# Slot steps of a four-layer graph kernel: index rows by DMA from DRAM, all diagonals on ScalarE, the variance ahead of the second normalisation, two buffers of powers

## What is computed

```python
m_j = h @ W1[:D];  m_i = h @ W1[D:]
pre = m_j[:, None, :, :] + m_i[:, :, None, :] + b1          # for every pair i, j
msg = gelu(layernorm(pre, g1, be1))
agg = einsum('bijo,bij->bio', msg, adjacency)
out = layernorm(concat([h, agg]) @ W2 + b2, g2, be2)
```

## Time and profile before

| | us |
|---|---|
| median of 3 runs (4080.77 to 4090.16) | 4087.21 |
| the profiled execution, device time | 4083.3 |
| its span, first to last instruction | 4081.4 |

### The profile page before, as it was taken

One profiled execution on the slowest core, in us unless ns is written; L12 is line 12 of the kernel. 1 busy time (PEld: TensorE's weight loads), 2 busy tenths in 40 slices (PEclk: granted clock), 3 DMA queues, 4 the chain that ended last, 5 costly groups with the idle time before them and its releaser, 6 DMA issues.

```text
span 4081.4 us, 93269 instructions
## 1 busy us (share of the span) xinstructions
PE 3302.0 (81%) x25274; PEld 2780.7 (68%) x25556; DVE 3378.2 (83%) x12271; ACT 2785.5 (68%) x6381; POOL 2108.6 (52%) x1923
## 2 busy tenths in 40 slices
PE   3484688887888888888798888888887887988898
PEld 2273567677676777767677776767776676776777
DVE  4788888898888888888888888888898888887830
ACT  2484676858667586776858676685868768595753
POOL 1182663718547292753729274471827547192730
PEclk7596899989899999999999999999999999999999
DMA  2000001000010100001010000101000010000000
GB/s 81 26 1 26 1 1 42 1 22 21 1 43 1 43 0 22 22 1 43 1 35 9 22 22 1 43 1 43 0 22 22 1 43 1 27 0 1 16 1 21
DMA packets 95513, 73.89 MB, mean 18 GB/s; under 512 B 7504, under 2 KB 95184, under 8 KB 95184
## 3 DMA queue, kind: packets, MB, share of 16 engines
q1 hardware_dynamic: 95184, 70.09, 5.7%
HBM read 61.68 MB, written 8.39 MB: 17 GB/s over the span
## 4 chain that ended last, share of the span: by engine, by line
issue 26%; POOL 25%; DVE 21%; PE 16%; ACT 6%; DVEq 3%; POOLq 2%; ACTq 0%; DMA 0%; SPq 0%
POOL v_z L511 18%; POOL v_diag L517 3%; PE n_bank_d L1599 3%; PE n_bank_d L1600 3%; PE n_bank_c L1582 3%; DVE v_normed L971 2%; PE n_bank_d L1596 2%; POOL v_prstd L525 2%; DVE v_top_at L1043 2%; PE n_bank_b L1660 1%; DVE v_top L1040 1%; PE n_bank_d L1496 1%; ACT v_pair L842 1%; DVE v_adj_x L1048 1%; POOLq L532 1%
## 5 line engine op out<-in xcount | busy, mean ns | idle before, releaser
L511 POOL TENSOR_TENSOR v_z<-v_z,all_bc_L_gnn_be 128x512 f32<-128x512 f32 x620 | 786.2, 1269 | 22.0 <-DVE v_z L1093 22.0
L525 POOL TENSOR_TENSOR v_prstd<-v_pvar,all_neg_half 128x8 f32<-128x8 f32 x310 | 563.5, 1818 | 267.8 <-DVE v_pvar L1109 240.0
L1496 PE MATMUL n_bank_d<-v_diag,v_msg 128*128 128x128 f32 x4960 | 637.1, 284 | 32.2 <-ACT v_diag L740 32.2
L1496 PEld LDWEIGHTS n_bank_d<-v_diag,v_msg 128*128 128x128 f32 x4960 | 594.8, 197 | 35.2 <-ACT v_diag L740 35.2
L740 ACT ACTIVATE v_diag<-all_ident,v_value 128x128 f32<-128x128 f32 x1860 | 572.5, 386 | 0.0
L1485 PE MATMUL n_bank_b<-v_parts,v_onehot 128*128 128x128 f16 x5472 | 374.0, 224 | 152.6 <-ACT n_bank_b L682 152.6
L1485 PEld LDWEIGHTS n_bank_b<-v_parts,v_onehot 128*128 128x128 f16 x5472 | 332.7, 100 | 224.7 <-ACT n_bank_b L682 183.5
L1582 PE MATMUL n_bank_c<-all_l_wsd,v_fT 128*128 128x256 f32 x1792 | 449.1, 392 | 31.4 <-ACT v_adjT L667 28.9
L1485 PE MATMUL n_bank_c<-v_parts,v_onehot 128*128 128x128 f16 x4960 | 346.9, 226 | 141.7 <-ACT n_bank_c L682 141.6
L1485 PEld LDWEIGHTS n_bank_c<-v_parts,v_onehot 128*128 128x128 f16 x4960 | 308.6, 101 | 213.2 <-ACT n_bank_c L682 168.4
L677 ACT ACTIVATE v_fT<-n_bank_d,all_l_c 128x256 f32<-128x256 f32 x256 | 119.7, 474 | 447.1 <-PE n_bank_d L1600 446.9
(11 more groups left out here) (281 smaller groups left out, 7344.6 us busy)
## 6 DMA issues: line engine op xcount, KB each, us to landing
v_adj_l<-in_adj SPq DMA_DIRECT2D x128, 256.0 KB, 3.7
v_adj_x<-in_adj SPq DMA_DIRECT2D x64, 256.0 KB, 3.4
v_ring<-in_x SPq DMA_DIRECT2D x16, 512.0 KB, 5.9
out_x<-v_xout SPq DMA_DIRECT2D x64, 128.0 KB, 2.0
w_wu<-in_L_gnn_wu SPq DMA_DIRECT2D x4, 192.0 KB, 2.5
all_W<-in_L_gnn_W SPq DMA_DIRECT2D x2, 128.0 KB, 4.3
w_raw<-in_L_gnn_ws SPq DMA_DIRECT2D x1, 192.0 KB, 3.0
w_raw<-in_L_gnn_wd SPq DMA_DIRECT2D x1, 192.0 KB, 3.1
```

The costliest lines, as they stand in the source:

```text
L511: nc.gpsimd.tensor_tensor(z[par][:, units], z[par][:, units], wide(bc["L2_gnn_be1"])[:, units], ALU.add).then_inc(sem["z_ready"], 1)
L525: nc.gpsimd.tensor_tensor(prstd[:], pvar[:], minus_half, ALU.pow).then_inc(sem["prstd_ready"], 1)
L1496: ins = nc.tensor.matmul(ps_agg[:, u // NB, (u % NB) * P:(u % NB + 1) * P], msg[par][:, u], diag[par][:, u], start=False, stop=False, skip ...
```

## The change

- `spread_out` on PE and `keep_spread` on ACT are gone. After the index is turned, ACT keeps one chunk in SBUF, and SP stores it to a DRAM tensor `slot_rows` (row k is the index row of slot k, 2 KB). For each slot SP loads that row onto all 128 partitions (256 KB written) into one of two buffers of `spread`. The first two are loaded in the mix stage, behind the loads for slot taking and ahead of those for layer 0; the others in the slot stage, each when `pick` of the slot just before it is done.
- All eight diagonals are made by ACT.
- `prstd` has two buffers, and DVE forms `pvar` ahead of the second half's normalisation.
- ACT's order: seed half 0, Gelu half 1 of the slot before, seed half 1, Gelu half 0, eight diagonals.

```diff
+            def spread_out(slot, par):
+                sp.dma_start(spread[:, par], slot_rows[bass.ds(slot, 1)].broadcast_to((P, UNITS * P)))\
+                    .then_inc(spread_in[par], 16)
+
+            def first_spreads(a, again):
...
+                with sp.Fori(0, chunks) as c:
+                    sp.wait_ge(sem["index_kept"], first + c + 2)
...
+                    sp.dma_start(slot_rows[bass.ds(c * P, P)], indexT[:]).then_inc(index_stored, 16)
...
+                sp.wait_ge(index_stored, sp.snap(stored) * 16 + 16)
...
+                for par in range(2):
+                    spread_out(par, par)
+
+            def slots(a):
...
+                with sp.Fori(1, pairs + 1) as i:
+                    for par in range(2):
+                        sp.wait_ge(sem["onehot_ready"], before + (i * 2 + par))
...
+                        spread_out(i * 2 + par, par)
...
             with sp.Fori(1, GROUPS - 3) as g:
                 mix(g)
+                slots(g + 1)
...
-                def pool_step(par, step, slot, first=False):
+                def pool_step(par, step, first=False):
                     if not first:
                         shift(1 - par, step, 0)
                     pool.wait_ge(sem["pvar_ready"], step + 1)
-                    nc.gpsimd.tensor_tensor(prstd[:], pvar[:], minus_half, ALU.pow).then_inc(sem["prstd_ready"], 1)
+                    nc.gpsimd.tensor_tensor(prstd[:, par], pvar[:], minus_half, ALU.pow).then_inc(sem["prstd_ready"], 1)
                     if not first:
                         shift(1 - par, step, 1)
-                        diagonals(1 - par, step, slot - 1)
...
-                    for u in range(BY_ACT):
+                    for u in range(UNITS):
                         ins = nc.scalar.activation(diag[par][:, u], ident[:], ACT.Copy,
                                                    scale=value[:, u, bass.ds(slot, 1)])
...
+                def act_step(par, step, slot, second=False):
+                    act.wait_ge(sem["z_made"], step * 2 + 1)
+                    seed(1 - par, 0)
+                    if not second:
                         gelu(par, act.snap(step - 1), 1)
+                    act.wait_ge(sem["z_made"], step * 2 + 2)
+                    seed(1 - par, 1)
+                    gelu(1 - par, step, 0)
+                    diagonals(1 - par, step, slot - 1)
...
             def pick(ahead, par):
-                dve.wait_ge(sem["spread_kept"], ahead + 1)
+                dve.wait_ge(spread_in[par], (ahead + (2 - par)) * 8)
...
-                        if not first:
+                        if half_ == 0 and not first:
                             dve.wait_ge(sem["prstd_ready"], step + 1)
-                            dve.wait_ge(sem["msg_ready"], step * 2 + (half_ + 1))
-                            normalise(1 - par, half_)
+                            dve.wait_ge(sem["msg_ready"], step * 2 + 1)
+                            normalise(1 - par, 0)
                     dve.wait_ge(sem["stats_done"], step * 2 + 2)
                     v.tensor_scalar(pvar[:].rearrange("p (q u) -> p q u", u=2), pstats[:, par, :, :, 2], 1.0 / D, UP * UP * LN_EPS,
                                     ALU.mult, ALU.add).then_inc(sem["pvar_ready"], 1)
+                    if not first:
+                        dve.wait_ge(sem["msg_ready"], step * 2 + 2)
+                        normalise(1 - par, 1)
                     pick(dve.snap(step + g * 2 + 2), par)
```

More of the change, by code:

```diff
@@ L214 @@
 HALF = UNITS // 2
-BY_ACT = 6
 LOWEST = -3.4028235e38
@@ L270, in network @@
         node_of = plan.sb("node_of", [P, NB])
-        spread = plan.sb("spread", [P, UNITS * P], BF16)
+        spread = plan.sb("spread", [P, 2, UNITS * P], BF16)
         junk = plan.sb("junk", [P, 2, N], BF16)
@@ L367, in network @@
         x_in = s.sem("x_in")
+        index_stored = s.sem("index_stored")
+        spread_in = [s.sem(f"spread_in{i}") for i in range(2)]
         adj_in = [s.sem(f"adj_in{b}") for b in range(GB)]
@@ L426, in mix @@
                     load_extract(g + 2)
+                if l1:
+                    first_spreads(g + 1, again)
                 if l0:
@@ L456, in _ @@
             load_x(1)
-            mix(-1, l3=False)
+            mix(-1, l3=False, again=False)
+            slots(0)
             mix(0, l3=False)
+            slots(1)
             with sp.Fori(1, GROUPS - 3) as g:
                 mix(g)
+                slots(g + 1)
             mix(GROUPS - 3, l0=False)
+            slots(GROUPS - 2)
             mix(GROUPS - 2, extract=False, l0=False)
-            mix(GROUPS - 1, extract=False, l0=False)
-            mix(GROUPS, extract=False, l0=False, refill=False)
+            slots(GROUPS - 1)
+            mix(GROUPS - 1, extract=False, l0=False, l1=False)
+            mix(GROUPS, extract=False, l0=False, refill=False, l1=False)
             for b in range(GB):
@@ L697, in keep_index @@
                     act.wait_ge(sem["index_turned"], first + c + 1)
-                    nc.scalar.activation(indexT[:, bass.ds(c, 1)].rearrange("p a n -> p (a n)"), ps_index,
-                                         ACT.Copy).then_inc(sem["index_kept"], 1)
+                    act.wait_ge(index_stored, (first + c) * 16 + 16)
+                    nc.scalar.activation(indexT[:], ps_index, ACT.Copy).then_inc(sem["index_kept"], 1)
                 act.reg_add(kept, kept, chunks)
             def start_slots(g, before):
-                first_ahead = act.snap(before + g * 2)
                 for i in range(2):
@@ L742, in diagonals @@
                     ins.then_inc(sem["diag_ready"], 1)
[L744 to L748, removed]
-                        gelu(par, act.snap(step - 1), 1)
-                    if not first:
[L751 to L757, removed]
+                def act_step(par, step, slot, second=False):
+                    act.wait_ge(sem["z_made"], step * 2 + 1)
+                    seed(1 - par, 0)
+                    if not second:
+                        gelu(par, act.snap(step - 1), 1)
+                    act.wait_ge(sem["z_made"], step * 2 + 2)
+                    seed(1 - par, 1)
+                    gelu(1 - par, step, 0)
+                    diagonals(1 - par, step, slot - 1)
                 act_step(1, act.snap(before + 1), 1, second=True)
@@ L1464, in layer0_out @@
                 ins.then_inc(sem["out_made"], 1)
[L1466 to L1471, removed]
             def slots(g):
@@ L1613, in turn_h @@
                 def turn_h():
-                    if u:
-                        pe.wait_ge(sem["spread_kept"], after + (g + 1) * 2)
-                        pe.wait_ge(sem["spread_made"], after + (g + 1) * 3)
                     for b in range(GB):
```

69 lines of the change are left out of this document (33 added, 36 removed).

## The result

The changed kernel takes 4117.22 us (median of 4 runs, 4115.8 to 4119.2) against 4085.97 for the kernel before (4 runs): a ratio of 1.0077, with a 95% interval of 1.0062 to 1.0092. It is slower by 0.8%, where I had forecast 4005. Its profiled execution spans 4115.2 us, 33.8 more than the 4081.4 of before; the mean granted clock is 0.906 instead of 0.923.

What follows compares the result with a forecast made beforehand. POOL was taken to set the 5.11 us slot step. Steady steps -115, slot-stage starts +39 and mix stage -6 made -82: span 3999, median 4005 us, against 4087.2 before; range 3962 to 4240.

Steps and rivals of the forecast that it cites:

- The steady step: Slot stages, power to power: falls from 5.11 to 4.65 us, saving 0.46 in about 251 steps, -115 us.
- DVE's sum of 4.57: DVE's work in one steady step: 4.46, or 4.57 with `pvar` waiting directly behind the second statistics.
- ACT's ring of 4.63: Two-step loop through DVE, ACT's seeds, Gelu and diagonals, PE's gather and four wakes: 9.3 us, 4.63 a step.
- rival 3: Steady step: without POOL's 0.71, ACT or DVE is exposed above the rings; 4055 to 4092 us; chance 0.08.
- p: Length of one steady slot step in us: 5.11 before, forecast 4.65, with bounds 4.58 to 4.72.
- POOL's ring: Steady-step loop: power, DVE wake, normalise half 0, POOL wake, shift up to the next power: 4.52 us.
- ACT's sum of 4.47: ACT's work in a steady step: 4.80, less the 0.91 spread copy, plus two diagonals of 0.29: 4.47.
- The start of a slot stage: Slot 2's row queues behind mix-stage loads: fourth power 3.2 us later in groups 2 to 13; +39 in all.
- The turns: From mix to slots: spread matmuls and copies leave PE's chain, about 0.35 in 16 groups: -6 us.
- L: Landing time of a slot's row load: 3.3 us forecast, bounds 2.6 to 5.4; hidden while under 3.35.
- Rivals 1 and 2: Row load becomes the step's bound, kernel slower (chance 0.22), or is partly seen, 4018 to 4090 us (chance 0.13).
- rival 1: Row load: 128 reads of one address, served one after another, become the step's bound; up to 4590 us; chance 0.22.

## Why the prediction was wrong

- **The steady step: 4.65 forecast, 4.90 measured.** The step that failed is DVE's sum of 4.57. It took `pvar` at 0.26 and moved it directly behind the second statistics, without asking what POOL does then. POOL's shift runs there in every step, and `pvar` is held to its end: 0.60 from start to start (1963.73 to 1964.33). 4.57 - 0.26 + 0.60 = 4.91, which is above ACT's ring of 4.63 and would have decided. That is rival 3, an engine above my rings, with p = 4.85 to 5.0 and a chance of 0.08; the mechanism I named for it (ACT's work colliding) was another.
- **Its rings.** Without that hold the step is 4.43 (statistics in PSUM), below all of mine, 4.52 to 4.65. There the power takes 1.65, not 1.81, which takes POOL's ring to 4.36, and `pvar` 0.08 from start to start, not 0.26 (in the earlier trace rows it was partly held already), which takes 0.09 a step off ACT's ring. Where the other 0.1 of that ring lies no run shows; its four wakes of 0.08 were assumed. ACT's sum of 4.47 was right: it is busy all of 4.43.
- **The start of a slot stage: mechanism right, mis-sized.** The row stands behind the adjacency and x loads, and DVE waits 6.63. The fourth power is 4.6 us later in groups 2 to 13 on average, not 3.2, and 3.2 in groups 14 and 15, not 0.5. Little is won back: in groups 2 to 13 the first distance is 5.1 longer on average, the next two together only 0.5 shorter. The gather behind the wait runs at the granted clock of 0.50 and takes 1.89 (1.07 in a steady step); I had counted on that, and what else eats the gain no run separates. +58.9 in all against +39, inside my bounds of +18 to +80 (the upper one is mis-added: 5.9 in 12 groups are 71).
- **Groups 0 and 1**: 0 forecast, -2.5 measured.
- **The turns: -6 forecast, +24.5 measured.** At full clock the going of the matmuls saves 0.5 (11.3 against 11.8; I had 0.35); with part of it at the lower level it costs 1.2. That clock is worth +10.7 here and may be chance of one execution. +14.8 lie at the end of the slot stage, which my sum had no term for, and they return each time.
- **The row load**: L = 3.1 against 3.3, hidden in every steady step. Rivals 1 and 2, 0.35 of the chance, were wrong. All of my 0.22 for slower stood on rival 1: the kernel came out slower by another way. Store and first loads in the mix stage are hidden, as costed.
- **The sum.** With the measured step, 251 x 0.21 = 53 instead of 115, the forecast would be 4067; with the starts of +58.9, 4087; the rest is the turns.

The wait put in at the start (78.6 us) alone is larger than what the steps gain (50.1). With the start at its upper bound of +80 and the step as forecast, the change would still have come out faster, and with the measured step alone too (4067). The errors in step and start together use up the gain (4087); what makes the kernel slower than before is the two ends of the mix stages.

## What to carry to other kernels

Before a small DVE operation is moved, look at what POOL does in the place it moves to: compare its longest rows with the ends of POOL's, and keep its input in PSUM if a bank is free. A load that takes the place of on-chip work inherits its queue: whatever SP issues in a mix stage stands ahead of the first loads of the slot stage behind it, so that load must be placed by hand, and the one after it too. A gain that rests on the clock of one place has to be judged on the whole span.

## What the runs showed of the hardware

- A DVE operation on 8 elements from SBUF takes 0.17 us with POOL idle (1903.60), 0.68 when it starts 0.62 into a 1.28 us addition of POOL (it ends 0.03 behind that addition in 294 of 294 cases), and 0.17 beside the same addition with its input in PSUM. A 1024-element comparison of 2-byte input is not held by POOL's power on 8 elements (0.87 against 0.88).
- One 2 KB DRAM row read by 128 partitions lands in 3.1 us, 128 different rows in 2.6.
- With two 512-column matmuls without use (0.59 us) the turn was 11.7 to 12.1 us ahead of every one of groups 2 to 13, where it had mixed 11.3 and 13.0; on the whole span that bought next to nothing: 4113.76 against 4117.22 us, in different sets of runs.
